# Second layer's cross-attention: maxima of single score tiles in a ring of three PSUM banks, value tiles in a fourth, the values weighed in two parts

## The chip, the cores and the metric

One Trainium2 chip (trn2), one of its cores. The kernel is one program that runs a two-layer decoder over a batch of four sequences. The metric is the device time of one execution in microseconds (us), lower is better. Engines are named as in the profile: PE is TensorE (PEld its weight loads), DVE VectorE, ACT ScalarE, POOL GpSimd, SP SyncE.

## The reference

The input x is 4 x 512 x 256. Each of two layers adds three parts to it, each applied to a layer norm of x: an attention part, a cross-attention over a context of 4 x 512 x 256, and a feed-forward part. The change lies in the second layer's cross-attention:

```
H = 16; E = D // H                       # D = 256, E = 16
q = (Q @ Wq + bq).reshape(B, L, H, E)    # Q: layer norm of x; B = 4, L = S = 512
k = (K @ Wk + bk).reshape(B, S, H, E)    # K = V = context
v = (V @ Wv + bv).reshape(B, S, H, E)
scale = 1.0 / np.sqrt(E)
scores = einsum('blhe,bshe->bhls', q, k)
A = softmax(scale * scores, axis=-1)
out = einsum('bhls,bshd->blhd', A, v).reshape(B, L, H * E)
return out @ We + be
```

All of it is float32.

## The kernel before, in words

Nothing schedules this kernel: each engine has its own program, written out by hand, and runs it in that order; between engines there are semaphores alone. A batch's second cross-attention is a stretch of some 75 us that comes four times, once for each batch `b`.

The 16 heads are worked in four groups `g` of four. `q4` and `k4` hold for each group a 128 x 512 tile in which head `j` of the group takes partitions 32j to 32j+31, of which 16 are its features, one is for the maximum, and the rest is zero. A matmul of one head is then 32 rows deep and uses one of TensorE's four row groups, so heads j = 0, 1 and heads j = 2, 3 lie on different row groups. Softmax needs the maximum over keys for each query. It is had in two rounds.

- *Maxima*, `scores_for_max(p)` on PE (its matmuls are L1248) and `row_max(p)` on DVE (L2278 for p < 8, L2281 from there). A pair `p` is two heads by 128 queries: two matmuls into two PSUM banks, 128 x 1024 together, and one DVE reduction over both, which leaves two columns in `row_neg`. A group has eight pairs.
- *Row tile*, `rows_of_max(g)` (L1260): four transposes turn the group's maxima into rows, and `add_rows(g)` (L2285) adds them to `q4`, so that the second product is score less maximum.
- *Scores less maximum*, `scores_less_max(v)` (L1273): two heads by 128 keys against all 512 queries, two banks, keys on the partitions. ACT takes exp of both at once (L1779) into one of eight buffers `pr1`. A group has eight steps `v`, and even and odd ones alternate between the heads 0, 1 and 2, 3.
- *Values*, `weigh_heads(g, kc)` (L1282): for a block of 128 keys, four matmuls, one per head, into 32 PSUM partitions each (one of four column tiles). Four such steps fill the group's tile `og`, sums of the weights included. ACT copies it out (`drain_o`, L1769), PE turns it (`flip`, L1291), DVE divides by the sums (`over_sums`, L2290 and L2292), and `flip_back` (L1299) turns two groups at once for the last product.

The order on PE is a loop over groups and eight steps. In groups 0 to 2 each step has `scores_less_max` of this group and then `scores_for_max` of the next group, whose pairs are swapped two by two by `_max_pair` so that the two always lie on different row groups. Behind the eight steps come three value steps, the row tile of the next group, a flip, and the fourth value step. Group 3 has no maxima left. Before the loop PE makes group 0's eight pairs of maxima alone.

PSUM has eight banks. The scores less maximum take banks 4 to 7, two at a time. The pairs of maxima take banks 0, 1 and 2, 3 in turn. The value tile of a group lies in bank 4, 6, 4 and 3 in turn, so the scores of the next group's second step wait until ACT has copied it out:

```
LBO = Lane(sig("og_tile"), sig("og_drained"), [bank[4], bank[6], bank[4], bank[3]], (("og", 4),))
...
if i == 1 and g > 0:
    w(LBO.drained, g)
elif v >= 2:
    w(p1_ready, v if i == 0 else v - 1)
```

`_cross_tiles()` is the written-out list of which tile (max, row, flip, back) lies in which banks. `Placed.fill` makes PE wait for the last earlier tile that shares a bank, `Placed.take` makes the reader wait until the tile is full.

## Time and profile before

| what | value |
|---|---|
| median of three runs | 2887.26 us |
| lowest and highest run | 2886.65 and 2894.19 us |
| the profiled execution's own time | 2881.14 us |
| its span, first to last instruction | 2879.3 us |
| mean granted TensorE clock | 0.943 |
| busy share of the span: PE, DVE, ACT, POOL | 91%, 50%, 38%, 24% |
| the four groups of one batch, first scores to last value step | 15.86, 14.35, 14.36, 13.63 us |

The profile shows one execution. Busy is the time in which an engine has an instruction in flight; PE's matmuls are pipelined and their ends are modelled. A row of the order of time merges instructions of one line that follow each other: start, length, engine, line, operation, shapes and count, and in brackets how long the engine had stood still before it and which instruction of which engine ended that. One matmul of float32 appears as two MATMUL records, called passes below.

### The profile page before, as it was taken

How to read it: one execution, taken by the hardware profiler on the slowest of the kernel's cores; microseconds unless marked ns; L12 is line 12 of the kernel's file. 1: busy time of each engine (PE TensorE's matmuls, PEld its weight loads, DVE VectorE, ACT ScalarE, POOL GpSimd, SP SyncE). 2: the span in 40 equal slices, each digit the busy share in tenths (PEclk: the TensorE clock that was granted, in tenths of full speed). 3: DMA queues.
4: the chain of work that ended last, by engine and by line, in shares of the span. 5: the costliest groups of instructions: out<-in, count | busy, mean ns of one | idle time of the engine just before them, and what ended most of it. 6: DMA issues, size and time to landing. Idle time of an engine off the chain costs nothing. (4 is left out here: it accounts for less than half of the span.)

```text
span 2879.3 us, 40099 instructions
## 1 busy us (share of the span) xinstructions
PE 2606.6 (91%) x16440; PEld 1565.0 (54%) x16441; DVE 1442.9 (50%) x2107; ACT 1087.1 (38%) x1885; POOL 681.6 (24%) x364
## 2 busy tenths in 40 slices
PE   7779999999999999999977987999999998599998
PEld 4356532854256532754326975455463554488887
DVE  5556337842677328853550114545555444744442
ACT  3664334822555325732422322434444444011111
POOL 0246015820557016730432011000000000012222
PEclk9979999999999999999988996999999998699999
DMA  5540001200031000300027971010010101144453
GB/s 201 200 188 31 0 1 57 103 1 1 1 121 38 1 0 15 137 8 1 1 72 262 346 260 32 8 23 23 1 38 8 23 8 45 62 151 158 156 166 97
DMA packets 62126, 219.25 MB, mean 76 GB/s; under 512 B 12293, under 2 KB 28122, under 8 KB 45178
## 3 DMA queue, kind: packets, MB, share of 16 engines
q1 hardware_dynamic: 45802, 187.39, 18.0%
q0 software_dynamic: 9568, 18.75, 2.7%
q10 hardware_dynamic: 6576, 10.57, 1.0%
q8 instruction: 130, 2.13, 0.3%
q14 instruction: 50, 0.41, 0.0%
HBM read 172.50 MB, written 39.99 MB: 74 GB/s over the span
## 5 line engine op out<-in xcount | busy, mean ns | idle before, releaser
L652 PE MATMUL psum<-arena 128*128 128x256 f32 (+7 forms) x4224 | 1093.4, 410 | 67.6 <-ACT arena L1521 11.5
L652 PEld LDWEIGHTS psum<-arena 128*128 128x128 f32 (+1 forms) x4224 | 677.8, 196 | 428.3 <-issue 312.1
L2480 POOL TENSOR_TENSOR arena<-arena 128x1024 f32<-128x1024 f32 x128 | 299.6, 2374 | 98.4 <-DVE arena L1986 83.4
L1986 DVE TENSOR_TENSOR_SCAN arena<-arena,psum 128x512 f32<-128x512 f32 x256 | 290.8, 1200 | 22.4 <-PE psum L793 14.5
L793 PEld LDWEIGHTS psum<-arena 128*128 128x128 f32 x2048 | 236.6, 193 | 49.3 <-ACT arena L1551 40.3
L793 PE MATMUL psum<-arena 128*128 128x128 f32 x2048 | 249.0, 279 | 2.0 <-issue 1.9
L2487 POOL TENSOR_TENSOR arena<-arena 128x1024 f32<-128x1024 f32 x32 | 75.9, 2373 | 656.2 <-ACT arena L1639 656.2
L2515 POOL DMA_INDIRECT arena<-xn,arena x32 | 31.6, 989 | 797.5 <-DVE arena L2422 790.8
L2080 DVE SCALAR_TENSOR_TENSOR arena<-psum,arena 128x1024 f32<-128x1024 f32 x128 | 156.8, 1243 | 80.5 <-PE psum L938 80.1
L1639 ACT ACTIVATE arena<-arena 128x1024 f32<-128x1024 f32 x128 | 146.7, 1146 | 110.1 <-DVE arena L2080 109.9
L1544 ACT ACTIVATE arena<-arena 128x512 f32<-128x512 f32 x256 | 163.0, 709 | 0.0
L1818 ACT ACTIVATE arena<-psum 128x256 f32<-128x256 f32 x128 | 49.1, 383 | 296.5 <-PE psum L652 296.5
L1779 ACT ACTIVATE arena<-psum 128x1024 f32<-128x1024 f32 x128 | 128.6, 1023 | 68.1 <-PE psum L1273 64.6
L2491 POOL TENSOR_TENSOR arena<-arena 128x1024 f32<-128x1024 f32 x64 | 151.3, 2365 | 10.1 <-ACT arena L1639 1.2
L949 PE MATMUL psum<-arena 128*64 128x512 f32 x512 | 138.2, 617 | 15.5 <-ACT arena L1639 7.4
L1273 PE MATMUL psum<-arena 32*128 32x512 f32 x512 | 138.7, 655 | 8.9 <-ACT arena L1779 5.7
L938 PE MATMUL psum<-arena 64*128 64x512 f32 x512 | 142.5, 638 | 2.7 <-ACT arena L1617 2.7
L1248 PE MATMUL psum<-arena 32*128 32x512 f32 x512 | 139.3, 680 | 5.3 <-DVE arena L2278 5.3
L2064 DVE RECIPROCAL arena<-arena 128x256 f32<-128x256 f32 x64 | 110.9, 1743 | 46.2 <-ACT arena L1631 46.2
L2281 DVE TENSOR_REDUCE arena<-psum 128x2 f32<-128x1024 f32 x96 | 113.6, 1222 | 26.3 <-PE psum L1248 23.2
L2445 DVE TENSOR_TENSOR arena<-arena,psum 128x256 f32<-128x256 f32 x128 | 53.9, 421 | 142.2 <-ACT arena L1818 141.0
L1438 PE MATMUL psum<-arena 128*128 128x256 f32 x512 | 116.0, 378 | 0.0
(292 smaller groups left out, 2989.0 us busy)
## 6 DMA issues: line engine op xcount, KB each, us to landing
arena<-in_W SPq DMA_DIRECT2D x46, 1024.0 KB
arena<-c_rows SPq DMA_DIRECT2D x32, 512.0 KB, 4.0
arena<-in_Wg SPq DMA_DIRECT2D x16, 1024.0 KB, 4.9
arena<-in_Wu SPq DMA_DIRECT2D x16, 1024.0 KB, 7.5
arena<-in_Wd SPq DMA_DIRECT2D x16, 1024.0 KB, 9.8
arena<-in_xT SPq DMA_DIRECT2D x8, 512.0 KB, 6.1
zs_all<-arena SPq DMA_DIRECT2D x4, 1024.0 KB, 3.9
ut_all<-arena SPq DMA_DIRECT2D x4, 1024.0 KB, 8.7
```

Of the source, the lines that this page charges most:

```text
L652: r = mm(dst, w, x, start=i == 0, stop=i == len(pairs) - 1)
L793: r = mm(bank[4 + c][:, q * P:(q + 1) * P], duT[:, q, c * P:(c + 1) * P], diag[n % 2][:, q, :], start=True, stop=True)
L938: i = mm(bank[2 + 2 * (u % SBUFS) + r], xkT[64 * r:64 * r + 64, hp, kc * P:(kc + 1) * P], xqT[64 * r:64 * r + 64, hp, :], start=True, stop ...
L949: i = mm(bank[0][64 * r:64 * r + 64, :], v1[:, kc, 2 * hp + r, :], t2[u % TBUFS][:, r, :], start=kc == 0, stop=kc == NC - 1)
L1248: r = mm(t[:, j - j0, :], q4[32 * j:32 * j + 32, g, qc * P:(qc + 1) * P], k4[32 * j:32 * j + 32, g, :], start=True, stop=True)
L1273: r = mm(bank[4 + 2 * ((i + g) % 2) + j % 2], k4[32 * j:32 * j + 32, g, kc * P:(kc + 1) * P], q4[32 * j:32 * j + 32, g, :], start=True, st ...
L1544: A_(dA[n % 2][:, c, :], dl[:, c, :], ACT.Exp, scale=aneg[:, c, n:n + 1]).then_inc(dA_ready.sem, 1)
L1639: A_(t2[u % TBUFS], rl[u % RBUFS], ACT.Square, scale=0.125, bias=vec[:, V_NB:V_NB + 1])\
L1986: V.tensor_tensor_scan(hs[n % 3][:, c, :], dA[n % 2][:, c, :], bank[4 + c], 0.0, ALU.mult, ALU.add)\
L2080: V.scalar_tensor_tensor(rl[u % RBUFS], t, minus_nb8, bound[:, kc, :].unsqueeze(1).broadcast_to([P, 2, L]), ALU.max, ALU.min).then_inc(rel ...
L2480: nc.gpsimd.tensor_tensor(h, h, c_all[:, n % CBUFS, :].unsqueeze(1).broadcast_to([P, 2, L]), ALU.mult)\
L2491: nc.gpsimd.tensor_tensor(t, t, t2[kc], ALU.add).then_inc(tsum_step.sem, 1)
```

## The change

It alters five things, all in this stage.

1. The maxima are made one head at a time: each matmul of a pair fills a bank of its own and signals by itself, and DVE reduces it by itself (128 x 512 into one column). There are 48 such tiles a batch where there were 24 of double size. Group 0's first eight pairs stay as they are.
2. All tiles of `_cross_tiles()` up to the last two go through banks 0, 1, 2 in turn.
3. The maxima run one pair ahead: pair 8 is made before the loop, and step `v` makes pair `v + 9`. `_max_pair` is gone. Group 2's last step makes none.
4. The value tile lies in bank 3 for every group. With it goes the wait of a group's second score step for its copy, and the first score step waits for one exp less.
5. Value steps 0 and 1 are issued behind step i = 5 of each group, each as soon as its own exps are there. Step 2 stays behind the eight steps, step 3 behind the row tile and the flip.

```
@@ _cross_tiles
-    order = [(("row", 0), (0, 1))]
-    for g in range(4):
-        for i in range(8):
-            if g < 3:
-                order.append((("max", _max_pair(g + 1, i)), (2 * (i % 2), 2)))
-            elif i in (2, 5):
-                order.append(((("flip", 2), (0, 1)) if i == 2 else (("back", 0), (1, 1))))
-        if g < 3:
-            order.append((("row", g + 1), (0, 1)))
-        if 0 < g < 3:
-            order.append((("flip", g - 1), (2, 1)))
-    return order + [(("flip", 3), (0, 1)), (("back", 1), (1, 1))]
-def _max_pair(g, i):
-    return 8 * g + (i ^ 1)
+    order = [("row", 0), ("max", 16), ("max", 17)]
+    for v in range(32):
+        g, i = v // 8, v % 8
+        order += [("max", u) for u in range(18 + 2 * v, min(20 + 2 * v, 64))]
+        if g == 3 and i in (2, 5):
+            order.append(("flip", 2) if i == 2 else ("back", 0))
+        if i == 7 and g < 3:
+            order.append(("row", g + 1))
+            if g > 0:
+                order.append(("flip", g - 1))
+    return [(tile, (n % 3, 1)) for n, tile in enumerate(order)] + [(("flip", 3), (0, 1)), (("back", 1), (1, 1))]
@@ banks
-        LBO = Lane(sig("og_tile"), sig("og_drained"), [bank[4], bank[6], bank[4], bank[3]], (("og", 4),))
+        LBO = Lane(sig("og_tile"), sig("og_drained"), bank[3:4], (("og", 4),))
@@ PE, scores_for_max, p >= 8
-                        t = LBM.fill(pe, b, ("max", p))
-                    for j in (j0, j0 + 1):
-                        r = mm(t[:, j - j0, :], ...)
-                    r.then_inc((s1_full if p < 8 else LBM.full).sem, 1)
+                        for j in (j0, j0 + 1):
+                            t = LBM.fill(pe, b, ("max", 2 * p + j - j0))
+                            mm(t, ...).then_inc(LBM.full.sem, 1)
@@ PE, rows_of_max
-                        w(LBM.drained, LBM.upto(("max", _max_pair(g, 7))))
+                        w(LBM.drained, LBM.upto(("max", LH * g + LH - 1)))
@@ PE, scores_less_max
-                    if i == 1 and g > 0:
-                        w(LBO.drained, g)
-                    elif v >= 2:
-                        w(p1_ready, v if i == 0 else v - 1)
+                    if v >= 2:
+                        w(p1_ready, v - 1)
-                        r = mm(bank[4 + 2 * ((i + g) % 2) + j % 2], ...)
+                        r = mm(bank[4 + 2 * (v % 2) + j % 2], ...)
@@ PE, weigh_heads
-                    w(p1_ready, 8 * g + (8 if kc == NC - 1 else 7))
-                    t = LBO.fill(pe, b, "og", g) if kc == 0 else LBO.banks[g]
+                    w(p1_ready, 8 * g + 2 * kc + 2)
+                    t = LBO.fill(pe, b, "og", g) if kc == 0 else LBO.banks[0]
@@ PE, order of the stage
                 rows_of_max(0)
+                scores_for_max(8)
                 for g in range(4):
                     for i in range(8):
-                        scores_less_max(8 * g + i)
-                        if g < 3:
-                            scores_for_max(_max_pair(g + 1, i))
-                        elif i == 2:
+                        v = 8 * g + i
+                        scores_less_max(v)
+                        if v + 9 < V1:
+                            scores_for_max(v + 9)
+                        if g == 3 and i == 2:
                             flip(2)
-                        elif i == 5:
+                        if i == 5:
+                            weigh_heads(g, 0)
+                            weigh_heads(g, 1)
+                        if g == 3 and i == 5:
                             flip_back(0)
-                    for kc in range(NC - 1):
-                        weigh_heads(g, kc)
+                    weigh_heads(g, 2)
                     if g < 3:
                         rows_of_max(g + 1)
@@ DVE, row_max, p >= 8
-                        t = LBM.take(dve, b, ("max", p))
-                        V.reduce_max(at, t, AX.X, negate=True).then_inc(LBM.drained.sem, 1)
+                        for j in (j0, j0 + 1):
+                            t = LBM.take(dve, b, ("max", 2 * p + j - j0))
+                            V.reduce_max(at[:, j - j0:j - j0 + 1], t, AX.X, negate=True).then_inc(LBM.drained.sem, 1)
@@ DVE, order of the stage
                 add_rows(0)
+                row_max(8)
                 for g in range(3):
                     for i in range(8):
-                        row_max(_max_pair(g + 1, i))
+                        if 8 * g + i + 9 < V1:
+                            row_max(8 * g + i + 9)
```

ACT's program changes only in the banks that it reads (`pair = 4 + 2 * (v % 2)`).

How this moves PE's instructions, at the end of group 1 of a batch. In the rows L1273 is a matmul of the scores less maximum, L1248 one of the maxima, L1282 one of the values, L1260 a transpose of the row tile; what it waits for stands behind it: p1_ready is an exp, md_drained a reduction or another reader of `_cross_tiles()`, og_drained the copy of the value tile. Before, from the last score step on:

```order
L1273 MATMUL psum<-arena 128x512 [waits p1_ready]
L1273 MATMUL psum<-arena 128x512
L1248 MATMUL psum<-arena 128x512 [waits md_drained]
L1248 MATMUL psum<-arena 128x512
L1282 MATMUL psum<-arena 32x512 [waits p1_ready]
L1282 MATMUL psum<-arena 32x512 x3
L1282 MATMUL psum<-arena 32x512 [waits p1_ready]
L1282 MATMUL psum<-arena 32x512 x3
L1282 MATMUL psum<-arena 32x512 [waits p1_ready]
L1282 MATMUL psum<-arena 32x512 x3
L1260 MATMUL psum<-arena 128x128 [waits md_drained]
L1260 MATMUL psum<-arena 128x128 x3
```

Now, from the sixth score step (i = 5) on; in the changed kernel the same four are L1269, L1247, L1278 and L1258:

```order
L1269 MATMUL psum<-arena 128x512 [waits p1_ready]
L1269 MATMUL psum<-arena 128x512
L1247 MATMUL psum<-arena 128x512 [waits md_drained] x2
L1278 MATMUL psum<-arena 32x512 [waits og_drained,p1_ready]
L1278 MATMUL psum<-arena 32x512 x3
L1278 MATMUL psum<-arena 32x512 [waits p1_ready]
L1278 MATMUL psum<-arena 32x512 x3
L1269 MATMUL psum<-arena 128x512 [waits p1_ready]
L1269 MATMUL psum<-arena 128x512
L1247 MATMUL psum<-arena 128x512 [waits md_drained] x2
```

Two value steps have moved from behind the eight score steps to between the sixth and the seventh; each matmul of the maxima now has a wait of its own.

The head of the stage on PE, before:

```order
L1260 MATMUL psum<-arena 128x128 [waits s1_max,act_drained]
L1260 MATMUL psum<-arena 128x128 x3
L1273 MATMUL psum<-arena 128x512 [waits md_drained]
L1273 MATMUL psum<-arena 128x512
L1248 MATMUL psum<-arena 128x512 [waits md_drained]
L1248 MATMUL psum<-arena 128x512
```

and now:

```order
L1258 MATMUL psum<-arena 128x128 [waits s1_max,act_drained]
L1258 MATMUL psum<-arena 128x128 x3
L1247 MATMUL psum<-arena 128x512 x2
L1269 MATMUL psum<-arena 128x512 [waits md_drained]
L1269 MATMUL psum<-arena 128x512
L1247 MATMUL psum<-arena 128x512 [waits md_drained] x2
```

Pair 8 has moved ahead of the first score step, with no wait, behind the transposes of group 0's row tile.

## Rows read from the trace of the kernel before

**Rows 1.** The page: busy time of the engines, and the chain that ended last.
```profile
PE 2606.6 (91%) x16440; PEld 1565.0 (54%) x16441; DVE 1442.9 (50%) x2107; ACT 1087.1 (38%) x1885; POOL 681.6 (24%) x364
...
PE 31%; DVE 3%; DMA 1%; ACT 1%; issue 1%; SPq 0%; POOL 0%; POOLq 0%; another core or an unknown queue 0%; DVEq 0%
```
**Rows 2.** Windows by group, second batch: us, busy of PE, PEld, DVE, ACT, POOL, PEclk, DMA share.
```profile
2008.50:2024.36 15.86, 15.72 (x101) 6.40 (x101) 10.21 (x9) 8.18 (x8) 0.00 (x0) 0.82 0.00 1
2024.36:2038.71 14.35, 14.10 (x108) 6.17 (x104) 10.71 (x11) 8.68 (x9) 0.00 (x0) 1.00 0.00 0
2038.71:2053.07 14.36, 14.11 (x109) 6.18 (x105) 10.71 (x11) 8.68 (x9) 0.00 (x0) 1.00 0.00 1
2053.07:2066.70 13.63, 12.26 (x77) 4.16 (x73) 1.37 (x3) 8.46 (x9) 0.00 (x0) 1.00 0.00 1
```
**Rows 3.** DVE in order of time, groups 1 and 2 of the second batch.
```profile
2025.59 9.73 DVE L2281 TENSOR_REDUCE arena<-psum 128x2 f32<-128x1024 f32 x8 [1.44 <-PE psum L1248]
2037.38 0.69 DVE L2285 TENSOR_TENSOR arena<-arena,psum 128x512 f32<-128x512 f32 x1 [2.07 <-PE psum L1260]
2037.99 0.25 DVE L2290 RECIPROCAL arena<-psum 128x16 f32<-128x16 f32 x1
2038.27 0.42 DVE L2292 TENSOR_TENSOR arena<-psum,arena 128x256 f32<-128x256 f32 x1
2039.95 9.73 DVE L2281 TENSOR_REDUCE arena<-psum 128x2 f32<-128x1024 f32 x8 [1.25 <-PE psum L1248]
```
**Rows 4.** PE in order of time, group 1: two steps, then its end.
```profile
2030.29 0.59 PE L1273 MATMUL psum<-arena 32*128 32x512 f32 x2
2030.46 0.70 PE L1248 MATMUL psum<-arena 32*128 32x512 f32 x2
2030.72 0.59 PE L1273 MATMUL psum<-arena 32*128 32x512 f32 x2
2030.99 0.59 PE L1248 MATMUL psum<-arena 32*128 32x512 f32 x2
...
2033.45 0.59 PE L1248 MATMUL psum<-arena 32*128 32x512 f32 x2
2033.98 2.78 PE L1282 MATMUL psum<-arena 128*32 128x512 f32 x24
2036.69 0.66 PE L1260 MATMUL psum<-arena 128*128 128x128 f32 x4
...
2037.71 1.07 PE L1282 MATMUL psum<-arena 128*32 128x512 f32 x8
2038.71 0.70 PE L1273 MATMUL psum<-arena 32*128 32x512 f32 x2
```
**Rows 5.** ACT in order of time, group 3: exps 1 and 2, 6, 7 and 8.
```profile
2054.24 1.94 ACT L1779 ACTIVATE arena<-psum 128x1024 f32<-128x1024 f32 x2 [0.44 <-PE psum L1273]
...
2060.39 1.02 ACT L1779 ACTIVATE arena<-psum 128x1024 f32<-128x1024 f32 x1 [0.31 <-PE psum L1273]
2062.04 1.94 ACT L1779 ACTIVATE arena<-psum 128x1024 f32<-128x1024 f32 x2 [0.62 <-PE psum L1273]
```
**Rows 6.** PE in order of time, group 3: its four value steps.
```profile
2063.11 3.64 PE L1282 MATMUL psum<-arena 128*32 128x512 f32 x32 [0.52 <-ACT arena L1779]
```
**Rows 7.** Groups by line and form, DVE: busy us, mean ns of one.
```profile
L2281 DVE TENSOR_REDUCE arena<-psum 128x2 f32<-128x1024 f32 x96 | 113.6, 1222 | 26.3 <-PE psum L1248 23.2
...
L2014 DVE TENSOR_REDUCE arena<-psum 128x1 f32<-128x512 f32 x16 | 11.0, 686 | 18.3 <-PE psum L856 18.3
```
**Rows 8.** PE in order of time, head of the stage, second batch.
```profile
2006.99 0.77 PE L1260 MATMUL psum<-arena 128*128 128x128 f32 x4 [1.42 <-DVE arena L2278]
2008.54 1.22 PE L1273 MATMUL psum<-arena 32*128 32x512 f32 x2 [0.78 <-DVE arena L2285]
...
2009.55 1.06 PE L1273 MATMUL psum<-arena 32*128 32x512 f32 x2
...
2010.42 1.06 PE L1273 MATMUL psum<-arena 32*128 32x512 f32 x2
```

More of the change, by code:

```diff
@@ L1244, in scores_for_max @@
                         t = psum[:, 4 + j0:6 + j0, :]
-                    else:
-                        t = LBM.fill(pe, b, ("max", p))
-                    for j in (j0, j0 + 1):
-                        r = mm(t[:, j - j0, :], q4[32 * j:32 * j + 32, g, qc * P:(qc + 1) * P], k4[32 * j:32 * j + 32, g, :],
-                               start=True, stop=True)
-                    r.then_inc((s1_full if p < 8 else LBM.full).sem, 1)
+                        for j in (j0, j0 + 1):
+                            r = mm(t[:, j - j0, :], q4[32 * j:32 * j + 32, g, qc * P:(qc + 1) * P],
+                                   k4[32 * j:32 * j + 32, g, :], start=True, stop=True)
+                        r.then_inc(s1_full.sem, 1)
+                    else:
+                        for j in (j0, j0 + 1):
+                            t = LBM.fill(pe, b, ("max", 2 * p + j - j0))
+                            mm(t, q4[32 * j:32 * j + 32, g, qc * P:(qc + 1) * P], k4[32 * j:32 * j + 32, g, :],
+                               start=True, stop=True).then_inc(LBM.full.sem, 1)
                 def rows_of_max(g):
@@ L1267, in scores_less_max @@
                         w(LBM.drained, LBM.upto(("row", g)))
-                    if i == 1 and g > 0:
-                        w(LBO.drained, g)
-                    elif v >= 2:
-                        w(p1_ready, v if i == 0 else v - 1)
+                    if v >= 2:
+                        w(p1_ready, v - 1)
                     for j in (j0, j0 + 1):
-                        r = mm(bank[4 + 2 * ((i + g) % 2) + j % 2], k4[32 * j:32 * j + 32, g, kc * P:(kc + 1) * P],
+                        r = mm(bank[4 + 2 * (v % 2) + j % 2], k4[32 * j:32 * j + 32, g, kc * P:(kc + 1) * P],
                                q4[32 * j:32 * j + 32, g, :], start=True, stop=True)
@@ L1773, in _ @@
                     g, i = v // 8, v % 8
-                    pair = 4 + 2 * ((i + g) % 2)
+                    pair = 4 + 2 * (v % 2)
                     w(s2_full, v + 1)
@@ L2279, in row_max @@
                     else:
-                        t = LBM.take(dve, b, ("max", p))
-                        V.reduce_max(at, t, AX.X, negate=True).then_inc(LBM.drained.sem, 1)
+                        for j in (j0, j0 + 1):
+                            t = LBM.take(dve, b, ("max", 2 * p + j - j0))
+                            V.reduce_max(at[:, j - j0:j - j0 + 1], t, AX.X, negate=True).then_inc(LBM.drained.sem, 1)
                 def add_rows(g):
```

## The prediction

> **What bounds the kernel now.** Read the page's shares first: PE is busy 91% of the span [rows 1], a modelled figure for pipelined matmuls, so it does not say what limits this stage. The windows by head group do [rows 2]: in one batch the second cross-attention's four groups take 15.86, 14.35, 14.36 and 13.63 us, 58.2 in all. The first has a granted TensorE clock of 0.82 (part of it at 1.2 GHz), the others 1.00 (2.4 GHz). Next the DVE's order of time [rows 3]: in groups 0 to 2, eight L2281 reductions run end to end, 9.73 us for 8, or 1.216 a step, with no gap. The vector engine paces those steps. Then it stands still while PE weighs the values: from 2035.32 (2025.59 + 9.73) to the next reduction at 2039.95 pass 4.63 us, which hold 2.07 of waiting for the row tile, about 1.3 of work (L2285, L2290, L2292) and 1.25 of waiting for the first scores. PE's order of time [rows 4] has what it does meanwhile: three value steps from 2033.98 to the row transposes at 2036.69 (2.71, so 0.90 each), then the transposes, then the fourth value step, 1.00 until the next scores. In group 3, which has no reductions, ACT and PE alternate [rows 5, 6].
>
> **The change, by step of one batch.** All of it lies on the path, because in each step either DVE or the PE-ACT alternation is what ends last.
>
> *Reductions.* One of 128x1024 takes 1222 ns; the same operation on 128x512 from PSUM into one column, L2014, takes 686 [rows 7]. Two of those are 1.372 against 1.216 in the present flow: +0.156 a pair, +1.25 for a group of 8 pairs.
>
> *Value halves in the middle of a group.* After the sixth score step PE gets two value steps, 1.81 us. The ring holds three single tiles. PE refills a bank as soon as its reduction ends, so at that moment DVE holds three tiles of work, 3 x 0.686 = 2.06. PE needs 0.1 for the handover and 1.12 for the single (first pass at 2030.46, second at 2030.99 for 0.59 [rows 4]), 1.81 for the values and 1.06 for the next single, less 0.13 of overlap at the two borders: 3.96. DVE idles 3.96 - 2.06 = **1.9 us**. Bounds: 0 if the lead covered all, 2.5 if the mode borders cost more.
>
> *Row tile.* At a group's end DVE is a pair ahead. The last single is filled while three tiles are left (2.06); PE does 1.22 - 0.07 for it, 0.90 for one value step and 0.69 from row transposes to L2285's start (2036.69 to 2037.38): 2.74. DVE waits 0.7 where it waited 2.07: **-1.4**. This is the intended gain. The border after it (fourth value step, first scores) is as before, -0.1 because one tile instead of two must be full.
>
> A full group (group 1): +1.25 + 1.9 - 1.4 - 0.1 = **+1.65**. Group 2 has seven pairs left, 14 x 0.686 = 9.60 against 9.73 (-0.13); its last two singles are filled together and the row tile then waits for the last score pair too, 0.95 instead of 2.07 (-1.1): -0.13 + 1.9 - 1.1 - 0.1 = **+0.55**.
>
> *Group 0* runs its first steps at the lower clock; there a PE step is about 1.7 us and hides some of the longer reductions, so I take **+1.5**, bounds 0.4 (no reduction shows) and 2. Ahead of it, the pre-filled pair 8 uses the same two row groups as the first score step. At this clock passes follow each other every 0.87 (2009.55 to 2010.42), two of them 1.7, while the score step, which waits for L2285, starts 0.78 after the transposes end (2007.76 to 2008.54) [rows 8]. It would now start 1.7 after them, rounded down **0.8** later (nothing if the clock were up, where two passes take 0.86).
>
> *Group 3.* Two value steps leave the tail and one more is hidden behind the last exp: from the end of exp 7 of 8 the group took 3.64 [rows 6]; now it is the last exp 1.02, the handover 0.15 and one value step 1.0, so -1.5. In the middle, between exps 6 and 7, the gap was 0.62 [rows 5]; now PE has 1.81 more to do before the next scores: +1.7. Sum **+0.2**. That the second score step of a group no longer waits for og_drained gains nothing: ACT already takes the first two exps back to back, 1.94 for 2 [rows 5].
>
> *At nothing:* each single waits for the reduction three tiles before, and behind it in PE's queue stand the next scores and so ACT's next exp. ACT then gets work every 1.37 us and needs 1.02 for it (1.94 for 2 end to end), 8.2 to 8.7 busy of some 14 [rows 2, 5], so that queue costs nothing within the steps. The wait goes to DVE's pace, not to ACT's. The stage moves no DMA: its share is 0.00 [rows 2].
>
> Sum: 0.8 + 1.5 + 1.65 + 0.55 + 0.2 = **+4.7 us a batch**, four batches (96 L2281 = 4 x 24): **+18.8**. The profiled execution took 2881.1 (span 2879.3), so it would take 2899.9. The median of the runs, 2887.3, lies 6.1 above that execution; on its scale the change gives **2906**. About 0.3% (8.7 us) is what a measurement of this kernel can tell from no change.
>
> **A rule weighed.** Across row groups the rows show overlap that is not in order: two first passes of L1273 start at 2030.29, two first passes of L1248 at 2030.46, and only then the second passes, at 2030.72 and 2030.99 [rows 4]. So a single on one row group does not hold up the scores behind it on another, and I let each row group run by itself. The Trainium skill ("TensorE: Matmul & The Clock Gate", Part 3: Packing small matmuls) says instead that matmuls start and end strictly in program order; by that, the second pass of each matmul would hold back all behind it. It gives the third rival below.
>
> The added value halves also add one more switch from row to column tiles and back in each group. The rows have such a border at 0.53 us from start to start (2033.45 to 2033.98) against 0.43 within a mode (2030.29 to 2030.72) [rows 4], and that is in my sum. The Trainium skill ("TensorEngine Tiling (Array Packing)", Key Properties) says that changing the mode drains TensorE, which speaks against this change; it gives no figure.
>
> **The rivals.**
> 1. *The lead covers the halves: no loss.* If DVE never ran dry at the value halves, 3 x 1.9 = 5.7 go, and a batch changes by 4.7 - 5.7 = -1.0: 2906 - 22.8 = 2883, no measurable change. It decides where PE's 3.96 us of tile, values and tile fit into the reductions in store. For it: ACT and DVE both have more to do per step than PE. Against: three banks are 2.06 us, less than the 2.7 that even the tile and the two values take.
> 2. *The clock falls.* PE's density goes down, 108 matmul records in 14.35 us [rows 2] to 108 in 16.0. If groups 1 and 2 ran at 1.2 GHz, 16 steps at about 1.7 instead of 1.37 add 5.3, and 8 value steps at double time 7.2: +12.5 a batch, +50: 2956; if only the low stretch in group 0 were as long again, it costs once more what it costs now (15.86 - 14.35 = 1.5), +6: 2912. Against: group 3 has 77 records in 13.63 us and keeps 1.00 [rows 2].
> 3. *Singles run one after the other.* If a single's two passes held back what is behind them, four matmuls of a step would take 4 x 0.43 = 1.72 instead of 1.37: 24 pairs x 0.35 = 8.4 a batch, +34: 2940. Against: the order of rows 4 just read.
> 4. *The lead does not do what it says.* If PE fell behind so far after the halves that the reductions left at a group's end hide nothing of the row tile, the -1.4, -1.4 and -1.1 of groups 0 to 2 go: 3.9 a batch, +16: 2922. For it: after the halves PE has two score steps and three singles to catch up on. Against: without a wait its step is below 1.22 [rows 3], DVE's new one 1.37.
>
> **How the numbers follow.** Forecast 0.70, with its own range 2896 to 2912 (+1.8 to +6.4 a batch: 1.9 between 1.4 and 2.5 in three groups, group 0's term between 0.4 and 2, the start between 0 and 0.8, not all at one end). Rival 1: 0.12. Rival 2: 0.06, mostly its small form. Rival 3: 0.05. Rival 4: 0.07. The range 2891 to 2922 leaves out rival 1's lower half and the large forms of 2 and 3, plus the edges. Faster by over 0.3% needs more than rival 1 gives: 0.04. Within: most of rival 1 and the low edge of the forecast, 0.13. Slower: 0.83.
>
> **What would show it.** The new L2282 reductions at about 686 ns, x192 in the program (4 batches of 48). Idle of DVE before L2282 waiting for L1247: once in each of groups 0 to 2 of about 1.9 us, just where two value steps stand in PE's order. The wait of L2286 for L1258 down from 2.07 to 0.7. Group windows of about 17.4, 16.0, 14.9 and 13.8 us. In group 3 one value step after the last exp, where four stood after the last but one. I am wrong if DVE's flow has no gap at the halves (rival 1), if the granted clock in groups 1 and 2 is under 1.00 (2), or if a step takes over 1.5 us inside a group (3).

## The result, and the profile after

| | before | after |
|---|---|---|
| median of the runs | 2888.8 us (2886.65 to 2894.19, 4 runs) | 2911.74 us (2906.76 to 2920.87, 4 runs) |
| ratio, 95% interval | | 1.0083 [1.0058, 1.0107] |
| the profiled execution's own time | 2881.14 us | 2909.96 us |
| span, mean granted clock | 2879.3 us, 0.943 | 2908.1 us, 0.945 |

The kernel is slower by 22.9 us between the medians. 2906 was forecast, with a range of 2891 to 2922. The profiled execution, 28.8 us over that of before, is slower by somewhat more.

The page of the changed kernel, busy time and the chain that ended last. PE's busy time and the shares of the chain hardly moved [rows 1]: nothing here tells where the time went.

```profile
PE 2631.5 (90%) x16440; PEld 1588.9 (55%) x16441; DVE 1453.8 (50%) x2203; ACT 1085.7 (37%) x1885; POOL 681.2 (23%) x364
...
PE 31%; DVE 2%; DMA 2%; issue 1%; ACT 1%; SPq 0%; POOL 0%; POOLq 0%; another core or an unknown queue 0%; DVEq 0%; ACTq 0%
```

The windows by group of the second batch, columns as in rows 2. Against 15.86, 14.35, 14.36 and 13.63 [rows 2] (group 3 is 13.69 by the single records, in all four batches) the groups now take:

```profile
2018.31:2036.04 17.73, 17.73 (x106) 8.78 (x100) 12.39 (x19) 7.97 (x8) 0.00 (x0) 0.89 0.00 1
2036.04:2052.56 16.52, 16.52 (x112) 7.99 (x108) 11.59 (x19) 8.56 (x9) 0.00 (x0) 1.00 0.00 0
2052.56:2067.99 15.43, 15.43 (x108) 7.66 (x104) 10.30 (x17) 8.57 (x9) 0.00 (x0) 1.00 0.00 1
2067.99:2081.88 13.89, 11.23 (x77) 3.47 (x74) 1.37 (x3) 8.46 (x9) 0.00 (x0) 1.00 0.00 1
```

The same four numbers within 0.5 us for group 0 and within 0.01 for the others stand in every batch. With the head (start of the row transposes to the first scores, read like the groups from the single records; 2.88 in three batches and 2.24 in the first, against 1.55 to 1.87 before) a batch's stage takes 66.2 to 66.4 us where it took 59.8 to 60.1. That is +6.5 a batch and 26 of the 28.8 us. The remaining 2.9 lie outside the stage, where the program is unchanged: 1.3 ahead of the first batch's, 1.0 between the first and the second, 0.6 behind the last. What moved there is open.

DVE in order of time from group 1's first maxima to group 2's row tile, to be read against rows 3:

```profile
2037.22 2.60 DVE L2282 TENSOR_REDUCE arena<-psum 128x1 f32<-128x512 f32 x4 [1.42 <-PE psum L1247]
2040.03 2.60 DVE L2282 TENSOR_REDUCE arena<-psum 128x1 f32<-128x512 f32 x4 [0.21 <-PE psum L1247]
2042.83 2.60 DVE L2282 TENSOR_REDUCE arena<-psum 128x1 f32<-128x512 f32 x4 [0.21 <-PE psum L1247]
2047.70 2.60 DVE L2282 TENSOR_REDUCE arena<-psum 128x1 f32<-128x512 f32 x4 [2.28 <-PE psum L1247]
2051.19 0.69 DVE L2286 TENSOR_TENSOR arena<-arena,psum 128x512 f32<-128x512 f32 x1 [0.89 <-PE psum L1258]
...
2053.74 2.60 DVE L2282 TENSOR_REDUCE arena<-psum 128x1 f32<-128x512 f32 x4 [1.23 <-PE psum L1247]
```

Three things are to be seen. The reductions no longer run as one block of 9.73 us. They come in fours, 2.60 each, with 0.21 between. In the middle of the group stands the gap of the value halves, 2.28. And the wait for the row tile fell from 2.07 to 0.89. (A block is merged by the profile; its length runs from the first start to the last end.)

PE at the value halves of group 1, and DVE and ACT just before them. The columns are those of rows 4.

```profile
2044.63 1.93 PE L1278 MATMUL psum<-arena 128*32 128x512 f32 x16
2046.49 0.70 PE L1269 MATMUL psum<-arena 32*128 32x512 f32 x2
2046.50 0.70 PE L1247 MATMUL psum<-arena 32*128 32x512 f32 x2
2047.02 0.59 PE L1269 MATMUL psum<-arena 32*128 32x512 f32 x2
2047.03 1.00 PE L1247 MATMUL psum<-arena 32*128 32x512 f32 x3
```

```profile
2041.23 1.39 DVE L2282 TENSOR_REDUCE arena<-psum 128x1 f32<-128x512 f32 x2
2041.37 0.69 PE L1247 MATMUL psum<-arena 32*128 32x512 f32 x1
2041.59 0.73 PE L1269 MATMUL psum<-arena 32*128 32x512 f32 x2
...
2041.90 0.76 PE L1247 MATMUL psum<-arena 32*128 32x512 f32 x2
...
2042.17 0.78 PE L1269 MATMUL psum<-arena 32*128 32x512 f32 x2
...
2042.79 1.02 ACT L1779 ACTIVATE arena<-psum 128x1024 f32<-128x1024 f32 x1 [0.59 <-PE psum L1269]
2042.83 0.69 DVE L2282 TENSOR_REDUCE arena<-psum 128x1 f32<-128x512 f32 x1 [0.21 <-PE psum L1247]
```

The first of the two views shows two value steps, sixteen records in 1.93 us, then scores and maxima together. DVE goes on only at 2047.70, when these end. The second view shows how a block of four reductions ends; it is read further down.

### The profile page after: what moved, and what is told of

Same layout as the page of the kernel before. It is cut to its first block and busy times, and to the rows that moved or that the text cites. A ratio compares the mean times of both kernels' runs of the same rounds, so it can differ in the third digit from the quotient of the medians.

```text
span 2908.1 us, 40207 instructions
## 1 busy us (share of the span) xinstructions
PE 2631.5 (90%) x16440; PEld 1588.9 (55%) x16441; DVE 1453.8 (50%) x2203; ACT 1085.7 (37%) x1885; POOL 681.2 (23%) x364
## 3 DMA queue, kind: packets, MB, share of 16 engines
q8 instruction: 130, 2.13, 0.3%
## 5 line engine op out<-in xcount | busy, mean ns | idle before, releaser
L1269 PE MATMUL psum<-arena 32*128 32x512 f32 x512 | 150.3, 645 | 6.5 <-ACT arena L1779 6.5
L2282 DVE TENSOR_REDUCE arena<-psum 128x1 f32<-128x512 f32 x192 | 124.2, 687 | 54.1 <-PE psum L1247 53.4
L1247 PE MATMUL psum<-arena 32*128 32x512 f32 x384 | 146.9, 694 | 0.0
```

What stands on the lines that cost most here:

```text
L1247: mm(t, q4[32 * j:32 * j + 32, g, qc * P:(qc + 1) * P], k4[32 * j:32 * j + 32, g, :], start=True, stop=True).then_inc(LBM.full.sem, 1)
L1269: r = mm(bank[4 + 2 * (v % 2) + j % 2], k4[32 * j:32 * j + 32, g, kc * P:(kc + 1) * P], q4[32 * j:32 * j + 32, g, :], start=True, stop=True)
```

## The experiments

All differ from one of the two kernels by the edit shown. "Head" and "group" are as above, read from the trace of each run's own profiled execution; where a time is given, the kernel before ran on the same chip beside it. The changed kernel did not, so the experiments that start from it are compared with it by their windows, which repeat in all four batches within 0.02 us for groups 1 and 2. Their medians are too near its own for that: ratios of 1.0077 to 1.0123 with intervals that overlap 1.0058 to 1.0107.

**The value steps back at the group's end.**

```
-                        if i == 5:
-                            weigh_heads(g, 0)
-                            weigh_heads(g, 1)
...
-                    weigh_heads(g, 2)
+                    for kc in range(3):
+                        weigh_heads(g, kc)
```

> The changed kernel with value steps 0 and 1 put back behind the eight score steps; all else as changed. Depth theory (the still time of DVE comes from the three single tiles that can be in store, wherever PE turns to the values): the 2.28 us gap inside groups 0 to 2 goes, and nearly as much comes back as a longer wait for the row tile; group 1 stays at 16.3 to 16.5 us, group 3 loses some 0.5; the program about 2 us shorter than the changed one. Split theory (the halves in the middle are an addition): each of groups 0 to 2 loses about 2.3 us, 27 us over the program, back to the time of the kernel before.

Measured: 2904.03 us (2903.73 to 2906.36) beside 2885.07, ratio 1.0077 [1.0058, 1.0096]. Group 1 took 16.17 us instead of 16.52, group 2 15.42 instead of 15.43, group 3 13.11 instead of 13.89. DVE, in order of time, around group 1:

```profile
2040.53 2.60 DVE L2280 TENSOR_REDUCE arena<-psum 128x1 f32<-128x512 f32 x4 [1.42 <-PE psum L1247]
2043.34 2.60 DVE L2280 TENSOR_REDUCE arena<-psum 128x1 f32<-128x512 f32 x4 [0.21 <-PE psum L1247]
2046.14 2.60 DVE L2280 TENSOR_REDUCE arena<-psum 128x1 f32<-128x512 f32 x4 [0.21 <-PE psum L1247]
2048.95 2.60 DVE L2280 TENSOR_REDUCE arena<-psum 128x1 f32<-128x512 f32 x4 [0.21 <-PE psum L1247]
2054.16 0.69 DVE L2284 TENSOR_TENSOR arena<-arena,psum 128x512 f32<-128x512 f32 x1 [2.61 <-PE psum L1258]
```

The gap inside the group is gone, and the wait for the row tile is back at 2.61, more than the kernel before had. The group got 0.35 us shorter, not 2.3, and somewhat shorter than the 16.3 to 16.5 of the depth theory. The split theory falls: the halves themselves cost 0.35 in group 1, nothing in group 2, and 0.78 in group 3.

PE in group 3 of this kernel, the four value steps behind the last scores:

```profile
2080.36 3.64 PE L1278 MATMUL psum<-arena 128*32 128x512 f32 x32
```

They last as long as in the kernel before [rows 6], but the 0.52 of waiting for an exp ahead of them is gone. The changed kernel lets each value step wait for its own exps only, and this is what makes group 3 here 0.58 shorter than the 13.69 before, with all value steps at the end.

**No pair ahead.**

```
-    order = [("row", 0), ("max", 16), ("max", 17)]
+    order = [("row", 0)]
...
-                scores_for_max(8)
...
-                        if v + 9 < V1:
-                            scores_for_max(v + 9)
+                        if v + 8 < V1:
+                            scores_for_max(8 + (v ^ 1))
```

> The changed kernel without the pair ahead (pair 8 not before the loop, step v makes pair 8 + (v ^ 1)); ring of three and halves kept. Lead theory (as predicted: the lead takes 1.4 us from the wait for the row tile in each of groups 0 to 2): each of groups 0 and 1 gets 1.4 us longer, group 2 1.1 and one pair more; with 0.8 less at the head some 14 us more over the program. Depth theory (the lead does not change how long PE works alone between the last tile it fills and the next group's first): group 1 stays within 0.2 us of 16.52, group 2 becomes as long as group 1 (it has eight pairs again, +1.1), the head 0.8 to 1.7 shorter: the program within 3 us of the changed one.

Measured: 2916.05 us (2912.70 to 2924.83) beside 2885.07, ratio 1.0123 [1.0096, 1.0149]. Groups 1 and 2 took 16.52 each, the head 1.78 to 1.87, a batch 66.8 to 67.4. DVE in group 1 of the second batch:

```profile
2047.97 2.60 DVE L2281 TENSOR_REDUCE arena<-psum 128x1 f32<-128x512 f32 x4 [0.21 <-PE psum L1247]
2052.85 2.60 DVE L2281 TENSOR_REDUCE arena<-psum 128x1 f32<-128x512 f32 x4 [2.27 <-PE psum L1247]
2056.34 0.69 DVE L2285 TENSOR_TENSOR arena<-arena,psum 128x512 f32<-128x512 f32 x1 [0.89 <-PE psum L1258]
```

The wait for the row tile is 0.89 here too, without any lead. So the lead was not what brought it down from 2.07, and it is worth nothing within a group: 16.52 with it and without it. What the lead does is to move one pair from group 2 to the head: with it group 2 is 1.09 shorter and the head 1.0 longer. A batch is even 0.7 longer without the lead (2.8 over the four stages, as the depth theory allowed), and that lies in group 0, 18.1 to 18.6 against 17.7 to 18.2, whose first steps run at the lower clock. The lead theory falls.

**A ring of four banks, value tiles and steps as before.**

```
-    return [(tile, (n % 3, 1)) for n, tile in enumerate(order)] + ...
+    places = [(tile, (n % 4, 1)) for n, tile in enumerate(order[:last])]
...
-        LBO = Lane(sig("og_tile"), sig("og_drained"), bank[3:4], (("og", 4),))
+        LBO = Lane(sig("og_tile"), sig("og_drained"), [bank[4], bank[6], bank[4], bank[3]], (("og", 4),))
```

(with the waits and places of value and score tiles of the kernel before, and its value steps at the end)

> Single tiles and the pair ahead kept, but a ring of four banks, value tiles in banks 4, 6, 4, 3 and all value steps at the group's end as before. Depth theory: with four banks the singles come every 0.61 us, two steps in 2.5 or less, group 1 14.8 to 15.0 us; the program 4 to 8 us above the kernel before, the rest from the head of the stage. Reduction theory (a 128x512 reduction costs 0.69 however it is fed): 16 of them take 11.0 us, group 1 at least 15.6 us, the program 16 us or more above the kernel before.

Measured: 2883.56 us (2879.54 to 2890.61, 10 runs) beside 2885.07, ratio 1.0001 [0.9988, 1.0013]: no change against the kernel before. Group 1 14.33, group 2 13.99, group 3 13.69, head 2.88 in three batches. DVE around group 1:

```profile
2028.33 9.66 DVE L2285 TENSOR_REDUCE arena<-psum 128x1 f32<-128x512 f32 x16 [1.42 <-PE psum L1250]
2040.12 0.69 DVE L2289 TENSOR_TENSOR arena<-arena,psum 128x512 f32<-128x512 f32 x1 [2.13 <-PE psum L1261]
```

Sixteen single reductions take 9.66 us, no more than eight double ones (9.73). A single lasts 0.69, but with the next bank full the following one starts some 0.60 after it ((9.66 - 0.69) / 15). The depth theory had expected more, 14.8 to 15.0 for group 1 and a program 4 to 8 us above the kernel before. The reduction theory falls, and with it the +1.25 of the prediction: in this flow single maxima cost nothing.

That they cost nothing is not all DVE's doing. In the single records of the kernel before, the eight double reductions start alternately 1.14 and 1.31 apart, and each one that comes 1.31 after the last starts 0.02 behind the signal of its tile. So DVE waited for PE there every second time, without a gap that the merged row shows. Its own pace for a double is 1.14, and two singles at 0.60 are 0.06 more.

From this kernel to the one with the value steps at the end and a ring of three, group 1 goes from 14.33 to 16.17 and group 2 from 13.99 to 15.42. That 1.84 is the price of the fourth bank, given to the value tiles, together with the waits that this spares the scores; the two were not tried apart. It adds up from the two traces within 0.02: reductions 9.66 to 11.03 (four times 2.60 and three times 0.21), row tile wait 2.13 to 2.61.

**Scores between the two singles.**

```
+                        if v + 9 < V1:
+                            scores_for_max(v + 9, 0)
                         scores_less_max(v)
                         if v + 9 < V1:
-                            scores_for_max(v + 9)
+                            scores_for_max(v + 9, 1)
```

> The changed kernel with the step's order on PE altered: first single of the pair, then the two score matmuls, then the second single. Completion theory (a single's signal comes only when the score matmuls issued before it are done too, and these are late because one of them waits for the row group of the single before): the scores no longer start behind a just issued single on their own row group, the two-step beat falls from 2.81 to some 2.6, group 1 from 16.52 to about 16.05, the program 5 to 6 us shorter than the changed one. Ring theory alone (each row group signals by itself, three banks set the beat): nothing is held back now, so nothing is won; group 1 0.2 us longer or unchanged, the program 0 to 3 us longer.

Measured: 2908.33 us (2899.66 to 2916.47) beside 2885.07, ratio 1.0085 [1.0052, 1.0117]. Groups 0 to 2 fell to 16.7 to 17.0, 15.79 and 14.76, group 1 by 0.73. But group 3 rose to 16.58. DVE in group 1, and the windows by group of the second batch:

```profile
2037.76 7.60 DVE L2284 TENSOR_REDUCE arena<-psum 128x1 f32<-128x512 f32 x12 [1.36 <-PE psum L1247]
2047.58 2.60 DVE L2284 TENSOR_REDUCE arena<-psum 128x1 f32<-128x512 f32 x4 [2.21 <-PE psum L1247]
2051.07 0.69 DVE L2288 TENSOR_TENSOR arena<-arena,psum 128x512 f32<-128x512 f32 x1 [0.89 <-PE psum L1258]
```

```profile
2019.86:2036.70 16.84, 16.84 (x106) 7.58 (x100) 12.10 (x19) 7.98 (x8) 0.00 (x0) 0.88 0.00 1
2036.70:2052.49 15.79, 15.79 (x108) 6.67 (x108) 11.41 (x19) 8.58 (x9) 0.00 (x0) 1.00 0.00 0
2052.49:2067.25 14.76, 14.76 (x104) 6.37 (x104) 10.12 (x17) 8.58 (x9) 0.00 (x0) 1.00 0.00 1
2067.25:2083.83 16.58, 14.42 (x73) 4.05 (x74) 1.37 (x3) 8.60 (x10) 0.00 (x0) 0.79 0.00 1
```

Twelve reductions now run end to end in 7.60 where they took three times 2.60 and two gaps, 8.22. So the 0.21 gaps were no matter of ring depth alone, and the completion theory said right what goes. Group 1 got shorter by more than it forecast, 0.73 for 0.47. The last window has a granted clock of 0.79: beginning 54.4 to 55.0 us after the start of the row transposes, PE ran at 1.2 GHz for 6.8 us, in all four batches. That cost 2.7 us a batch and took back the 2.1 to 2.9 gained in groups 0 to 2.

**The two value steps apart.**

```
-                        if i == 5:
-                            weigh_heads(g, 0)
-                            weigh_heads(g, 1)
+                        if i in (3, 5):
+                            weigh_heads(g, (i - 3) // 2)
```

> The changed kernel with its two value steps apart: step 0 behind score step i = 3, step 1 behind i = 5. Depth theory: each makes a gap of its own, because fill 1.22, one value step 0.90 and the next fill 1.06 less 0.13 are 3.05 us of PE and the three tiles in store are 1.8 us of reductions: two gaps of 1.2 in place of one of 2.28; group 1 16.5 to 16.8 us. Cover theory (what is as short as 0.9 us fits into the store): no gap, group 1 at 14.3 to 14.6, the program 20 us shorter than the changed one. Group 3: 13.89 falls to about 13.0 in both, one value step then lies beside an exp.

Measured: 2909.72 us in one execution, beside 2879.81. Group 1 16.87, group 2 15.78. DVE in group 1:

```profile
2037.45 2.60 DVE L2281 TENSOR_REDUCE arena<-psum 128x1 f32<-128x512 f32 x4 [1.42 <-PE psum L1247]
2040.26 2.60 DVE L2281 TENSOR_REDUCE arena<-psum 128x1 f32<-128x512 f32 x4 [0.21 <-PE psum L1247]
2044.27 2.60 DVE L2281 TENSOR_REDUCE arena<-psum 128x1 f32<-128x512 f32 x4 [1.42 <-PE psum L1247]
2048.28 2.60 DVE L2281 TENSOR_REDUCE arena<-psum 128x1 f32<-128x512 f32 x4 [1.42 <-PE psum L1247]
2051.77 0.69 DVE L2285 TENSOR_TENSOR arena<-arena,psum 128x512 f32<-128x512 f32 x1 [0.89 <-PE psum L1258]
```

Each single value step makes a gap of its own, 1.42, twice in place of 2.28 and one 0.21. That is more than the 1.2 each that the depth theory expected, and the group a little longer than its 16.5 to 16.8. The cover theory falls: with three banks even 0.9 us of values do not fit. Group 3 took 13.02 in the first batch. In the others the granted clock was at its lower level for 3.4 us, from 4.6 us behind the group's start on, and it took 14.43.

**The kernel before, with one value step of group 3 earlier.** The edit has a second part: in group 3 each value step now waits for its own exps only.

```
-                    w(p1_ready, 8 * g + (8 if kc == NC - 1 else 7))
+                    w(p1_ready, 8 * g + (2 * kc + 2 if g == 3 else 8 if kc == NC - 1 else 7))
...
                         elif i == 2:
                             flip(2)
+                        elif i == 4:
+                            weigh_heads(3, 0)
...
-                    for kc in range(NC - 1):
+                    for kc in range(NC - 1) if g < 3 else (1, 2):
```

> The kernel before with one edit: in group 3, whose value tile lies in bank 3 already, value step 0 is issued behind the fifth score step. Cover theory: one value step (0.9 us) lies beside an exp there and leaves the tail; group 3 falls from 13.70 to 12.8 or so, 3.5 to 4 us over the program. Rival (PE is busy there, the step only pushes the next scores and exps back): group 3 unchanged, the program too.

Measured: 2875.87 us (2872.23 to 2884.63, 10 runs) beside 2881.87, ratio 0.9985 [0.9972, 0.9999]. Group 3 took 12.65 instead of 13.69, in every batch. PE in group 3:

```profile
2054.30 1.73 PE L1273 MATMUL psum<-arena 32*128 32x512 f32 x8
2055.97 1.07 PE L1282 MATMUL psum<-arena 128*32 128x512 f32 x8
2056.96 1.13 PE L1273 MATMUL psum<-arena 32*128 32x512 f32 x4
...
2060.27 2.78 PE L1282 MATMUL psum<-arena 128*32 128x512 f32 x24
```

The step at 2055.97 is followed by the next scores at 2056.96 without a wait, where the kernel before let PE wait 0.52 us for an exp. Three value steps instead of four are left at the end, 2.78 against 3.64 [rows 6]. But the gain of 1.04 is not all theirs. These three start 1.06 after the last score step does, where the four of the kernel before started 1.64 after it and waited 0.52 for an exp: 0.59 comes from the second part of the edit alone, as much as in group 3 of the first experiment. The moved step gives the rest: 0.86 less at the end, 0.41 more in the middle, where the next scores start that much later. The cover theory holds for half of the step.

**Ring of four without the pair ahead.** On the kernel of the third experiment:

```
-                scores_for_max(8)
...
-                        if v + 9 < V1:
-                            scores_for_max(v + 9)
+                        if v + 8 < V1:
+                            scores_for_max(8 + (v ^ 1))
```

> The kernel with the ring of four without the pair ahead. Depth theory (the lead is worth nothing): groups 1 and 2 both 14.3 to 14.4 us, the head 1.9 instead of 2.9, a batch from the first row transposes to the last value step 59.0 to 59.4 us (59.9 before): the program 2 to 3 us below the kernel before. Lead theory: the wait for the row tile grows from 2.12 by a pair's 1.2 us and so does each group, 15.5 us; the program 10 us or more above the kernel before.

Measured: 2879.76 us (2875.47 to 2893.05, 10 runs) beside 2881.87, ratio 1.0003 [0.9987, 1.0019]. Groups 1 and 2 14.33 each, head 1.87: the lead is worth nothing here either. But group 0 took 15.63 to 15.86 where the kernel with the lead had 14.68 to 15.13, so a batch came to 59.8 to 60.1, not 59.0 to 59.4. What the lead loses at the head, 1.0, it gains in group 0 and, 0.34, in group 2.

**Ring of four, pair 8 ahead of the row tile.**

```
-    order = [("row", 0), ("max", 16), ("max", 17)]
+    order = [("max", 16), ("max", 17), ("row", 0)]
...
-                rows_of_max(0)
                 scores_for_max(8)
+                rows_of_max(0)
```

> The kernel with the ring of four, but pair 8 is made before group 0's row tile, while PE waits for group 0's last maxima, and reduced before the row tile is added. Head theory (the head is late only because pair 8 lies on the first score step's row groups, at the low clock): the head falls from 2.88 to 1.9 or less, all groups as with the ring of four; the program 3 to 4 us below the kernel before. Rival (the extra two reductions push the row tile's addition back as much): head 2.5 or more, the program as the kernel before.

Measured: 2881.16 us (2868.80 to 2887.97, 10 runs) beside 2881.87, ratio 0.9993 [0.9978, 1.0008]. The head fell to 1.79 to 1.90. In the profiled execution (2868.8 us) three of the four stages had no stretch at the lower clock. Group 0 of the second and of the fourth batch (the windows begin 0.2 us ahead of its first scores):

```profile
2004.07:2017.96 13.89, 13.38 (x100) 6.15 (x100) 10.49 (x18) 8.08 (x8) 0.00 (x0) 1.00 0.00 1
2346.14:2361.69 15.55, 15.35 (x100) 6.64 (x100) 10.68 (x18) 8.08 (x8) 0.00 (x0) 0.84 0.01 1
```

The same instructions take 13.89 at full clock and 15.55 where it is half for a while. The head theory holds for the head. Whether the program gains is below what ten runs tell, because the clock at the head of the stage is given or not from one batch to the next. The three shortest runs (2868.8 to 2872.2) have the highest mean granted clocks of the ten, 0.948 to 0.950 against 0.944 to 0.946.

**Both: ring of four with pair 8 early, and one value step of group 3 earlier.** To the kernel just shown comes, with the same change of group 3's waits as above,

```
+                        if g == 3 and i == 4:
+                            weigh_heads(3, 0)
...
-                    for kc in range(3):
+                    for kc in range(g // 3, 3):
```

> The last two edits together: ring of four, pair 8 before the row tile, value step 0 of group 3 behind its fifth score step. If they add up: a batch some 58.0 us, the program 7 to 8 us below the kernel before. If the granted clock falls in group 3 (it did in the kernel with the scores between the singles), group 3 gets 2 to 3 us longer instead and the gain is gone.

Measured: 2873.99 us (2870.26 to 2883.43, 12 runs) beside 2881.87, ratio 0.9983 [0.9971, 0.9995]. Groups 1 to 3 took 14.33, 13.99 and 12.65: the gains add up inside the stage. This is the best version with runs enough for an interval, 0.17% below the kernel before, and the one with the edit in group 3 alone (0.9985) cannot be told from it.

**The same with the scores between the singles.** To the kernel just shown comes

```
+                        if v + 9 < V1:
+                            scores_for_max(v + 9, 0)
                         scores_less_max(v)
                         if v + 9 < V1:
-                            scores_for_max(v + 9)
+                            scores_for_max(v + 9, 1)
```

> The kernel with the ring of four, pair 8 early and value step 0 early in group 3, with the step's order first single, scores, second single. Completion theory: with four banks the reductions already run end to end (16 in 9.66 us), so nothing held back is left to win: groups 1 and 2 at 14.33 and 13.99 within 0.1. Ring theory: the beat depends on the order in any ring, groups 0.5 or more shorter. The clock: if it falls in group 3 here too, the order of singles and scores has to do with it, and group 3 takes 15 us or more; else 12.7.

Measured: 2873.8 us in one execution, beside 2879.81. Groups 1 and 2 14.27 and 13.93, group 3 12.65 at full clock. With four banks the order of singles and scores matters by 0.06 in these, as the completion theory had it. In group 0 it matters more: at full clock it took 13.50, where it took 13.89 in the two kernels before this one.

## Why the prediction was right, and where it was not

The side was right and the time lay in the range: +18.8 was forecast, +22.9 came between the medians. Within a batch 4.7 was forecast and the trace has 6.5. That the sum came as near as this is in part luck, since two of the three large terms of a full group, reductions and row tile, have the wrong cause. By its own steps:

| step | forecast | measured | |
|---|---|---|---|
| head | +0.8 | +1.0 to +1.3, in the first batch +0.4 | right, its cause shown by making pair 8 earlier |
| group 0 | +1.5 | +1.9 to +2.3 | undersized; with four banks it took 14.7 to 15.1, with three and the values at the end 17.1 to 17.8 |
| group 1 | +1.65 | +2.17 | undersized, two terms wrong in kind |
| group 2 | +0.55 | +1.08 | the same |
| group 3 | +0.2 | +0.2 (13.69 to 13.89) | right: the middle gap grew by 1.86 (1.7 forecast), the tail shrank by 1.66 (1.5) |

*Reductions, forecast +1.25 a group.* Measured: four times 2.60 is 10.40, against 9.73, and two gaps of 0.21: +1.09. The number is near by luck. The duration 686 ns was right (L2282: 687), but it is not what one costs in a flow: next bank full, they start 0.60 apart, and sixteen take 9.66. The step took a duration for a pace. What lengthened the flow instead is a term that the prediction put at nothing: that each single waits for the reduction three tiles before. In the single records of group 1 the starts of four reductions are 0.61, 0.60 and 0.70 apart and the next four begin 0.90 after the last. The 0.70 and the 0.90 are waits for a signal: DVE starts 0.02 behind it. Beside 0.60 that is 0.4 in each four.

*Value halves, forecast +1.9.* Measured 2.28. The working was right. The store is three tiles at 0.60, 1.8, where 2.06 was taken, the same slip of duration for pace; 3.96 - 1.8 is 2.16, and what the other 0.12 are is open.

*Row tile, forecast -1.4, "the intended gain".* DVE's wait there fell by 1.18, so the sign was right and the size near. The step that failed is the sentence before it, that DVE waits less because it "is a pair ahead". Without the lead the wait is the same 0.89 and the group the same 16.52. The wait is shorter because two of three value steps no longer stand in front of the row tile, and it comes back as the gap where they stand now: 2.28 + 0.89 = 3.17 with the halves, 2.61 + 0.21 = 2.82 without. The two terms were right as rows and wrong as causes, gain and loss of one move of PE's work. The loss that the halves leave is 0.35.

So the halves, the largest cost in the forecast, were not the main one. From kernel to kernel group 1's +2.17 is made of -0.02 for single maxima and a lead in four banks (14.35 to 14.33), +1.84 for taking the fourth bank from the ring and giving it to the value tiles (14.33 to 16.17), and +0.35 for the halves (16.17 to 16.52). The same path in group 2 is -0.36, +1.43 and +0.01, in group 3 0, -0.58 and +0.78. The waits that the value bank spares the scores are inside the second numbers; they were not tried apart.

*Rivals.* The first (the lead covers the halves) is out: three tiles are 1.8 us, and even one value step makes a gap. The fourth is right in that the lead is worth nothing inside a full group and wrong in its price, since the row tile's wait fell by the halves. The second, the clock, did not come in this kernel, groups 1 to 3 stand at 1.00, but it did in two of the experiments.

*The rule weighed.* The third rival's strong form, a step of 1.72, did not come: two steps take 2.81. Its mild form did. In the rows around 2042 of the trace after, the second pass of a single runs from 2041.90 for 0.59, to 2042.49 (single records; the rows merge two). DVE ended the reduction before at 2042.62 (2041.23 + 1.39), but started on that single only at 2042.83. The scores issued ahead of the single have their last pass from 2042.17 for 0.59, to 2042.76, and the exp that waits for them starts at 2042.79. So the single's signal came with the scores' end, 0.3 after its own. These were late because one of their heads had queued on the row group of the single before.

The times of the semaphore events, which the trace keeps beside the rows, say it directly: the scores signal at 2042.77 and the single, whose record ends at 2042.49, at 2042.81. This holds for every single of groups 1 and 2 in that batch. Either its signal comes 0.01 to 0.02 after its own end, or it comes 0.06 to 0.32 after it, and then always 0.04 behind the signal of scores issued ahead of it (0.09 where two singles follow one another there). With the first single issued ahead of the scores, no signal of groups 1 and 2 comes more than 0.10 after its own end. With a ring of four and the order as here, every second signal from the seventh of group 1 on is 0.16 to 0.30 late too, but DVE does not stand still, since another full bank is in store. So the 0.21 gaps take both, the late signal and the short ring.

The Trainium skill ("TensorE: Matmul & The Clock Gate", Part 3: Packing small matmuls) says that matmuls start and end strictly in program order. Of the two halves of that sentence this trace bears out one. The starts are not in order across row groups: a single starts at 2041.37, and three of the four passes of the two score matmuls that stand before it in the program start at 2041.59 or later. The completions, as the signals show them, are in order.

## What to carry to other kernels

Count a ring by what it stores at the reader's pace, not by the duration of one instruction. The pace is the distance from start to start where the next tile is already full; a merged row without a gap can still hold waits. Where PE works in order, its work apart from the ring costs its own length and the refill around it less that store, wherever it is put.

Before a bank is given from a ring to another use, ask what the ring's refill (here 1.2 us: 1.12 for the two passes and the handover) and the longest interruption need. Here the fourth bank was worth 1.84 us in group 1 and 1.43 in group 2, and the freedom that it bought, to issue values early, was worth nothing or less in each of the groups 1 to 3. In group 3 of the kernel before, where no ring runs, one value step behind the fifth score step gave some 0.45 us a batch, and 0.59 more came from letting each value step wait for no more than its own exps.

Where a signal is awaited, look at what was issued just ahead of the instruction that gives it: the signal can come as late as theirs.

## What the runs showed of the hardware

- Reductions from PSUM overlap: 128x512 lasts 686 ns, but with the next tile full they start 0.60 apart, sixteen in 9.66 us; 128x1024 lasts 1222 ns, and with the next tile full they start 1.14 apart.
- A matmul's signal does not come before that of the matmuls issued ahead of it on another row group: a single whose record ended at 2042.49 signalled at 2042.81, 0.04 behind the scores at 2042.77.
- The granted clock can fall where PE and ACT alternate: with the scores between the singles it was at its lower level for 6.8 us of group 3 in all four batches, with the values apart for 3.4 us in three. In the 4.4 us of group 3 ahead of the 6.8, PE had two score steps, 1.11 of waiting for an exp, a score step, four transposes and further scores, and it had the same in the changed kernel, where the clock stayed. What decides is open and was not tried. One and the same group 3 took 13.02 and 14.43.
- At the head of the stage the lower clock comes in most batches but not all: in 42 of the 48 stages of the twelve profiles. The six without it all lie in the three kernels that make pair 8 early, which have twelve stages; whether that edit is the cause was not tried. In the profile of the first of them it came in one batch of four, 13.89 against 15.55 for group 0. Some 1.7 us a batch hang on it, by estimate up to 6.6 an execution; that kernel's ten runs lie between 2868.80 and 2887.97, and an effect of 3 us can't be told among them.
